# One core, a fused attention and convolution kernel: a new order of work on all five engines

## What is computed

```python
x = x + attention(gn(x))      # gn: group norm over 32 groups of 4 channels
x = x + conv(gn(x))

# attention: linear attention, 4 heads of 32 channels
xn  = h / max(norm of h over channels, 1e-12) * g * sqrt(128)
q, k, v = split(w_qkv @ xn)
q = softmax(q, over the head's 32 channels) * 32 ** -0.5
k = softmax(concat(mem_k, k), over the 4 + 4096 pixels)
out = w_out @ ((k v^T) q) + b_out

# conv: a 3 x 3 convolution over the channel pairs with (j - i) % 4 == 0,
# plus a 1 x 1 convolution over all the other pairs, plus a bias
```

## Time and profile before

| | |
|---|---|
| median of 3 runs | 2064.62 us (2064.17 to 2066.17) |
| profiled execution, its time | 2065.06 us |
| its span, first to last instruction | 2063.2 us |
| mean granted TensorE clock | 0.983 |
| TensorE busy | 1913.9 us (93%) |
| VectorE busy | 1750.3 us (85%) |
| ScalarE busy | 1354.0 us (66%) |
| GpSimd busy | 1362.4 us (66%) |

### The profile page before, as it was taken

The page is one execution under the profiler, slowest core; times in us unless marked ns, Lnnn a source line. Parts: engine busy times, 40 slices in busy tenths (PEclk is TensorE's granted clock), DMA queues, the critical chain, the costliest instruction groups (busy, mean ns, idle before and its releaser), DMA issues.

```text
span 2063.2 us, 50607 instructions
## 1 busy us (share of the span) xinstructions
PE 1913.9 (93%) x21199; PEld 1013.4 (49%) x21199; DVE 1750.3 (85%) x3144; ACT 1354.0 (66%) x1476; POOL 1362.4 (66%) x737
## 2 busy tenths in 40 slices
PE   2889999999999999999999999999999999999996
PEld 0445445555445555444555544555544555554552
DVE  5689888888988888988888988888988888898863
ACT  2567666767667767667676766676766776766761
POOL 5566666766667766667676667676666676666762
PEclk9789999999999999999999999999999999999997
DMA  5357777887767887667787777778777778876665
GB/s 105 62 127 147 154 149 158 168 169 153 149 154 160 169 168 158 151 148 160 169 158 165 154 152 153 162 164 173 149 151 151 159 168 171 154 151 147 144 136 127
DMA packets 349427, 312.96 MB, mean 152 GB/s; under 512 B 299152, under 2 KB 299920, under 8 KB 341008
## 3 DMA queue, kind: packets, MB, share of 16 engines
q1 hardware_dynamic: 347712, 308.73, 72.1%
q10 hardware_dynamic: 1168, 0.98, 0.2%
q0 software_dynamic: 320, 0.01, 0.0%
HBM read 68.10 MB, written 67.11 MB: 66 GB/s over the span
## 4 chain that ended last, share of the span: by engine, by line
PE 45%; DVE 36%; ACT 12%; POOL 3%; issue 1%; DMA 1%; ACTq 0%; SPq 0%
PE pair_ps L765 8%; DVE km L1114 7%; DVE u L1111 7%; PE pair_ps L802 7%; PE pair_ps L745 5%; DVE image L1166 4%; DVE nrm L1101 4%; DVE parts L1101 3%; PE bank_ps L699 3%; POOL exp_kT_lo L447 3%; PE bank_ps L775 3%; PE pair_ps L768 3%; PE pair_ps L793 3%; DVE part L1100 2%; PE bank_ps L754 2%; PE bank_ps L757 2%
## 5 line engine op out<-in xcount | busy, mean ns | idle before, releaser
L802 PE MATMUL pair_ps<-replicas,w_rep 96*32 96x512 f16 x8192 | 488.9, 383 | 7.9 <-DMA replicas<-yg_lo 7.9
L444 POOL TENSOR_TENSOR u_lo<-u,u_hi 128x1024 f16<-128x1024 f32 x128 | 269.9, 2144 | 270.3 <-ACT u_hi L551 270.3
L447 POOL TENSOR_TENSOR exp_kT_lo<-exp_kT,exp_kT_hi 128x1024 f16<-128x1024 f32 x128 | 300.2, 2354 | 178.9 <-ACT exp_kT_hi L560 178.8
L802 PEld LDWEIGHTS pair_ps<-replicas,w_rep 96*32 96x32 f16 x8192 | 205.8, 96 | 263.2 <-issue 77.8
L450 POOL TENSOR_TENSOR u_lo<-exp_q,u_hi 128x1024 f16<-128x1024 f32 x128 | 272.7, 2143 | 88.8 <-ACT u_hi L566 85.3
L1166 DVE SCALAR_TENSOR_TENSOR image<-pair_ps,image 128x512 f32<-128x512 f32 x256 | 172.5, 682 | 123.5 <-PE pair_ps L802 119.8
L440 POOL TENSOR_SCALAR u<-image,st 128x1024 f32<-128x1024 f32 x128 | 187.4, 1475 | 109.2 <-DVE st L1065 109.2
L551 ACT ACTIVATE u_hi<-u 128x1024 f16<-128x1024 f32 x128 | 130.8, 1045 | 173.3 <-DVE u L1111 173.1
L557 ACT ACTIVATE exp_kT<-pair_ps,zcol 128x1024 f32<-128x1024 f32 x128 | 141.0, 1102 | 144.0 <-PE pair_ps L745 144.0
L566 ACT ACTIVATE u_hi<-exp_q 128x1024 f16<-128x1024 f32 x128 | 135.3, 1057 | 137.1 <-DVE exp_q L1153 130.5
L536 ACT ACTIVATE exp_kT<-u,zcol 128x1024 f32<-128x1024 f32 x128 | 146.0, 1143 | 93.2 <-POOL u L440 92.2
(11 more groups left out here) (179 smaller groups left out, 4716.5 us busy)
## 6 DMA issues: line engine op xcount, KB each, us to landing
image<-in_x SPq DMA_DIRECT2D x256, 256.0 KB, 4.8
out<-image SPq DMA_DIRECT2D x512, 128.0 KB, 2.2
replicas<-yg_hi SPq DMA_DIRECT2D x256, 165.0 KB, 3.9
replicas<-yg_hi SPq DMA_DIRECT2D x256, 107.2 KB, 5.1
replicas<-yg_lo SPq DMA_DIRECT2D x128, 165.0 KB, 4.4
replicas<-yg_lo SPq DMA_DIRECT2D x128, 107.2 KB, 3.8
uT_hi<-u_hi SPq DMA_TRANSPOSE x128, 3.4
uT_lo<-u_lo SPq DMA_TRANSPOSE x128, 3.4
```

Of the source, the lines that this page charges most:

```text
L444: pool.tensor_tensor(px(UL, v), px(U, v), px(UH, v), ALU.subtract).then_inc(ul_ready, 1)
L447: pool.tensor_tensor(KL[:, v % 2], KT[:, v % 2], KH[:, v % 2], ALU.subtract).then_inc(kl_ready, 1)
L802: mm = pe.matmul(conv_ps[32 * r:32 * r + 32, j % 2], w_rep[0:32 * SLOTS, tap, r], rep[:, j * ROWS + dy:(j + 1) * ROWS + dy, dx:dx + SIDE], ...
```

## The change

Only the order of the calls in the five `step` functions changes, with the waits and the choice of PSUM banks that go with it. No helper is altered, and the number of instructions per image is the same. The core of the diff, cut; image names as above.

TensorE, head of the step: `conv_ring` of chunk 5 comes over from the step before, `inv_norm(…, 2)` goes to the end of the step before, and `rough_q` 0 and 1 stand around `turn_k_max`.

```diff
             def step(p, a, c, e):
                 if a is not None:
-                    pe.wait_ge(u_ready, at(a, UNITS, 1))
-                    inv_norm(a, 2, pair_ps[0])
-                if e is not None:
-                    pe.wait_ge(out_ready, at(e, CHUNKS, 5))
-                    conv_dense(e, 6)
-                if a is not None:
                     pe.wait_ge(u_ready, at(a, UNITS, 2))
                     inv_norm(a, 3, pair_ps[1])
                 if e is not None:
-                    conv_ring(e, 6)
+                    conv_ring(e, 5)
...
+                    conv_ring(e, 6)
                 if a is not None:
                     pe.wait_ge(k_max, at(a, 8, 1))
                     pe.wait_ge(uh_ready, at(a, UNITS, 3))
                     rough_k(a, 2, pair_ps[0])
+                if e is not None:
+                    pe.wait_ge(out_ready, at(e, CHUNKS, 6))
+                    conv_dense(e, 7)
+                if a is not None:
                     pe.wait_ge(k_max, at(a, 8, 2))
                     pe.wait_ge(uh_ready, at(a, UNITS, 4))
                     rough_k(a, 3, pair_ps[1])
                 if e is not None:
                     conv_ring(e, 7)
                 if a is not None:
+                    pe.wait_ge(k_max, at(a, 8, 4))
+                    rough_q(a, 0, pair_ps[1])
                     pe.wait_ge(k_max, at(a, 8, 7))
-                    turn_k_max(bank_ps[0])
-                    rough_q(a, 0, pair_ps[1])
+                    turn_k_max(bank_ps[1])
+                    rough_q(a, 1, pair_ps[0])
+                    pe.wait_ge(ul_ready, at(a, UNITS, 1))
+                    pe.wait_ge(k_max, at(a, 8, 8))
+                    keys(a, 0, pair_ps[2])
```

TensorE, from the second group means to the end of the step (new lines and the kept ones between them; "..." for the rest):

```diff
+                    context(a, 3, bank_ps[0])
...
+                    pe.wait_ge(lo_even, at(c, UNITS // 2, 1))
+                    conv_dense(c, 0)
+                    conv_dense(c, 1)
...
+                    turn_context(bank_ps[1])
...
+                    pe.wait_ge(hi_in[0], at(c, 16 * 2 * RES, 16 * 2 * RES))
+                    pe.wait_ge(lo_in[0], at(c, 16 * RES, 16 * RES))
+                    conv_ring(c, 0)
+                    conv_ring(c, 1)
...
+                    pe.wait_ge(den_dve, at(a, 4, 4))
+                    den_broadcast(a, 0, pair_ps[1])
+                    den_broadcast(a, 1, pair_ps[0])
...
+                    pe.wait_ge(out_ready, at(c, CHUNKS, 1))
                     conv_dense(c, 2)
...
+                    value_context(bank_ps[0])
...
                     pe.wait_ge(sq_ready, at(p, UNITS, 1))
                     norm_sums(p, 0, bank_ps[1])
...
                     pe.wait_ge(sq_ready, at(p, UNITS, 2))
                     norm_sums(p, 1, bank_ps[1])
...
+                    pe.wait_ge(q_soft, at(a, UNITS, 2))
+                    den_broadcast(a, 2, pair_ps[0])
+                    den_broadcast(a, 3, pair_ps[1])
                     pe.wait_ge(mix_dve, at(a, 9, 7))
                     mix_weights(bank_ps[0])
...
+                    conv_ring(c, 2)
...
+                    conv_ring(c, 4)
...
+                    pe.wait_ge(norm_dve, at(p, 5, 5))
+                    inv_norm(p, 0, pair_ps[0])
...
+                    pe.wait_ge(out_ready, at(c, CHUNKS, 4))
+                    conv_dense(c, 5)
...
                     inv_norm(p, 1, pair_ps[1])
...
+                    pe.wait_ge(out_ready, at(c, CHUNKS, 5))
+                    conv_dense(c, 6)
...
+                    pe.wait_ge(u_ready, at(p, UNITS, 1))
+                    inv_norm(p, 2, pair_ps[0])
```

```diff
+                    dve.wait_ge(max_turned, at(a, 2, 2))
+                    rows_q(a, bank_ps[1])
                 if p is not None and not first(p):
                     dve.wait_ge(x_in[0][buffer_of(p)], at_load(p))
                     x_stats(p, 0)
-                if a is not None:
-                    dve.wait_ge(max_turned, at(a, 2, 2))
-                    rows_q(a, bank_ps[1])
+                    x_stats(p, 1)
+                    dve.wait_ge(x_in[1][buffer_of(p)], at_load(p))
+                    x_stats(p, 2)
+                    x_stats(p, 3)
                 if c is not None:
                     dve.wait_ge(hi_ready, at(c, UNITS, 1))
                     dve.wait_ge(yg_ready, at(c, UNITS, 1))
                     low_y(c, 0)
...
                     x_seed(p, bank_ps[1])
+                    dve.wait_ge(x_stat, at(p, X_STEPS, 8))
+                    x_scale(p)
```

ScalarE: the squares of image a's units 0 to 2 end the step; `high_y(c, 3)` stands behind `square(p, 0)`; `norm_log` stands ahead of `high_q(a, 3)`. GpSimd: `low_u` 0 ends the step before, all four `group_norm_y` come first, and `low_k(a, 2)` comes before `low_y(c, 1)`:

```diff
-                    pool.wait_ge(yg_ready, at(c, UNITS, 2))
-                    pool.wait_ge(hi_ready, at(c, UNITS, 2))
-                    low_y(c, 1)
+                    group_norm_y(c, 2)
+                    group_norm_y(c, 3)
                 if a is not None:
                     pool.wait_ge(kh_ready, at(a, UNITS, 3))
                     low_k(a, 2)
                 if c is not None:
-                    group_norm_y(c, 2)
+                    pool.wait_ge(hi_ready, at(c, UNITS, 2))
+                    pool.wait_ge(yg_ready, at(c, UNITS, 2))
+                    low_y(c, 1)
```

More of the change, by code:

```diff
@@ L368, in step @@
                 if a is not None:
+                    sp.wait_ge(ul_ready, at(a, UNITS, 2))
+                    turn_u(a, 1)
+                if p is not None and p >= PRELOADED:
+                    if e is not None:
+                        sp.wait_ge(stored[2], at(e, 16 * RES, 16 * RES))
+                    if e is not None:
+                        sp.wait_ge(stored[3], at(e, 16 * RES, 16 * RES))
+                    load(p, 1)
+                if a is not None:
                     sp.wait_ge(ul_ready, at(a, UNITS, 3))
                     turn_u(a, 2)
-                if p is not None and p >= PRELOADED:
-                    if e is not None:
-                        sp.wait_ge(stored[3], at(e, 16 * RES, 16 * RES))
-                    if e is not None:
-                        sp.wait_ge(stored[2], at(e, 16 * RES, 16 * RES))
-                    load(p, 1)
+                    sp.wait_ge(ul_ready, at(a, UNITS, 4))
+                    turn_u(a, 3)
                 if c is not None:
@@ L382, in step @@
                     replicate_low(c, 0)
-                if a is not None:
-                    sp.wait_ge(ul_ready, at(a, UNITS, 4))
-                    turn_u(a, 3)
-                if c is not None:
                     sp.wait_ge(hi_ready, at(c, UNITS, 4))
@@ L393, in step @@
                     store(c, 0)
+                    sp.wait_ge(out_ready, at(c, CHUNKS, 4))
+                    store(c, 1)
             over_samples(step, replicate_weights)
@@ L514, in step @@
                     low_q(a, 3)
+                if p is not None:
+                    pool.wait_ge(uh_ready, at(p, UNITS, 1))
+                    low_u(p, 0)
             over_samples(step)
@@ L639, in step @@
                     square(p, 0)
+                if c is not None:
+                    high_y(c, 3)
+                if p is not None:
                     act.wait_ge(xg_ready, at(p, UNITS, 2))
@@ L658, in step @@
                     high_q(a, 2)
+                if p is not None:
+                    act.wait_ge(norm_dve, at(p, 5, 1))
+                    norm_log()
+                if a is not None:
                     act.wait_ge(q_soft, at(a, UNITS, 4))
@@ L670, in step @@
                     square_y(a, 0)
+                    act.wait_ge(y_ready, at(a, UNITS, 2))
+                    square_y(a, 1)
+                    act.wait_ge(y_ready, at(a, UNITS, 3))
+                    square_y(a, 2)
+                if p is not None:
+                    act.wait_ge(u_ready, at(p, UNITS, 1))
+                    high_u(p, 0)
             act.wait_ge(setup_pe, 1)
@@ L867, in step @@
[L867 to L874 removed]
                     pe.wait_ge(kT_exp, at(a, UNITS, 1))
                     pe.wait_ge(ul_ready, at(a, UNITS, 3))
[L877 removed]
+                    keys(a, 2, pair_ps[2])
@@ L878, in step @@
+                    pe.wait_ge(q_max, at(a, 5, 3))
+                    rough_q(a, 3, pair_ps[1])
                     pe.wait_ge(kT_exp, at(a, UNITS, 2))
-                    rough_q(a, 2, pair_ps[2])
+                    pe.wait_ge(ul_ready, at(a, UNITS, 4))
+                    keys(a, 3, pair_ps[0])
+                    if c is not None:
+                        pe.wait_ge(y_stat, at(c, Y_STEPS, 9))
+                    pe.wait_ge(kl_ready, at(a, UNITS, 1))
                     pe.wait_ge(uT_in[0], at(a, 32, 32))
-                    pe.wait_ge(kl_ready, at(a, UNITS, 1))
@@ L1184, in step @@
                     max_k(a, 1, pair_ps[1])
+                if e is not None:
+                    dve.wait_ge(conv_done, at(e, CHUNKS, 7))
+                    finish(e, 6)
+                if a is not None:
                     dve.wait_ge(k_rough, at(a, UNITS, 3))
@@ L1190, in step @@
                     shift_k(a)
+                if e is not None:
+                    dve.wait_ge(conv_done, at(e, CHUNKS, 8))
+                    finish(e, 7)
+                if a is not None:
```

(15 more changed lines are left out.)

282 lines of the change are left out of this document (108 added, 174 removed).

## The result

| | before | after |
|---|---|---|
| median (runs) | 2065.39 us (4; 2064.17 to 2067.15) | 2013.02 us (4; 2011.28 to 2016.92) |
| profiled execution, its time | 2065.06 us | 2011.88 us |
| mean granted TensorE clock | 0.983 | 0.983 |

The ratio is 0.9748, 95% interval 0.9731 to 0.9766: 52 us faster, where 61 were forecast (2004 us, range 1980 to 2072). In the new kernel the lines of TensorE's and VectorE's helpers are 10 or 11 higher: `conv_ring` L813, `broadcast` L717, `norm_sums` L710, `turn_k_max` L822, `group_means` L819, `turn_context` L828, `low_y` L1171 on VectorE. GpSimd's are 3 lower: `low_y` L454.

What follows compares the result with a forecast made beforehand. TensorE's own work was taken as the floor: 57.5 us plus waits of 1.0, 0.3, 0.3 and 0.2 is 59.3, rounded-away parts make 59.4; gain 1.96 x 31 = 61 us, from 2065.06 to 2004 us, range 1980 to 2072.

Steps and rivals of the forecast that it cites:

- Work without waits, 57.5: TensorE's work per period: 61.36 less 3.3 of waits is 58.1, adjusted for new neighbours to 57.5 us.
- The joined `norm_sums`: On TensorE, norm_sums 0 and 1 become adjacent and one call is free: -1.0 us a period.
- A change of shape: Whole-array matmuls directly ahead of a group on part of the array: 0.1 us each, +0.4 a period, bounds 0 and 0.8.
- Four broadcasts run as one: Rival on TensorE's den_broadcast pairs: each adjacent pair gains 0.3 us, period 58.8, 1986 us; chance 0.18.
- Head of the step, 1.0: TensorE's waits before inv_norm 3 (0.5), the shift of the keys (0.25) and keys 0 (0.2): together 1.0 us a period.
- the shift of the keys: VectorE's shift_k, 1.2 us, ends its head chain at 11.65; TensorE, free at 11.4, waits 0.25 us.
- Low parts and the port: VectorE's low_y 0 runs 27.9 to 29.0, then GpSimd's low_y 1; group means possible at 29.7, wanted at 30.5: no wait.
- the rival 0.12: VectorE misses its turn: statistics end after 27.9, GpSimd goes first, group means +1.35 us; period 60.45, 2037 us; chance 0.12.
- Replicas, 0.3: Last replica of the first band lands at 37.3; TensorE is at ring 0 at 37.0: wait 0.3 us, bounds 0 and 2.5.
- `norm_sums` 3, 0.3: Second half of the step: square 3 is done at 47.3, TensorE is there at 47.0: wait 0.3 us.
- End, 0.2: VectorE has norm_parts, two finish and residual 3 between ring 3 and inv_norm 0: TensorE waits 0.2 us.
- The last image: Its convolution lies outside the 31 periods; order was said hardly to matter there, so no change was counted.

Runs made afterwards that it cites:

- e3: The changed kernel with x_moments ahead of low_y 0, and den_broadcast 1 and 3 moved apart from 0 and 2: 2021.91 us, ratio 0.9791 to before.
- e9: The changed kernel with x_moments first, low_y 0 between x_stats 1 and 2, transposes earlier on the queue, plus low_y 2 behind den_parts: 2074.86 us, 1.0042 of before.
- e10: The changed kernel with x_moments first, low_y 0 between x_stats 1 and 2, transposes earlier, plus ring 5 back in its own step: 2049.8 us, 0.994 of before.
- e5: The changed kernel with x_moments ahead of low_y 0, and GpSimd's second group norm waiting for weigh_context: 2025.78 us, ratio 0.9809 to before.
- e8: The changed kernel with x_moments first, low_y 0 between x_stats 1 and 2, transposes earlier, plus GpSimd's group_norm_x 1 waiting for weigh_context: 2029.18 us, 0.9815 of before.

## Why the prediction was right, and where its terms were off

The forecast was 9 us low. Its main mechanism was right: TensorE's old waits at the head of the step are gone, and what decides next are short waits at other places. The step that failed is the walk of the low parts at the port, and several terms of the sum were off both ways. By its own steps:

- *Work without waits, 57.5.* The joined `norm_sums` do run in 1.06, as it said. A change of shape does cost 0.1 (the slot of `mix` 2 ends at 338.58, ring 3 starts at 338.67). Four broadcasts run as one, which it charged in full: -0.6 (e3: +0.50 to undo it). That rival was right.
- *Head of the step, 1.0.* `inv_norm` 3 waits 0.55 (0.5 forecast); `turn_k_max` waits 0.0 (0.25) and `keys` 0 0.1 (0.2). I took 1.2 for the shift of the keys from the earlier trace rows, but in it stood a port wait: the instruction on two columns took 0.70 there, and takes 0.17 in after, where GpSimd is done by then. The term was 0.35 too high.
- *Low parts and the port.* "GpSimd's next began when VectorE's had ended" holds in 17 periods and fails in 13, at 1.36 each: 13 x 1.36 / 30 = +0.6 on the mean. With the broadcasts this is the largest error, and the one that made the forecast low. I gave the rival 0.12 and a condition, statistics later than 27.9; mostly they ended at 26.8, a us early, and it still happened. The condition explains 3 of the 13.
- *`turn_context`.* It has no term. `weigh_context` waits at the port, and ring 0 starts some 0.5 late.
- *Replicas, 0.3.* The last one lands at 37.1 on average where 37.3 was taken. Since ring 0 was late itself, it waits in 8 periods only, 0.13 on the mean of all.
- *`norm_sums` 3, 0.3.* It is 0.7: what four-as-one and the joined sums bring reaches `square` 3 as a wait.
- *End, 0.2.* There is none.
- *The last image* was counted at no change and took 2.7 us more; by the record its waits grew from 16.8 to 18.6 us, and the rest I did not follow up.

The steady period without a missed turn and without a wait for the replicas is then 59.4 - 0.6 - 0.35 + 0.5 + 0.4 - 0.3 - 0.2 = 58.85, which is what the shortest periods show. With 0.6 for the missed turns, 0.13 for the replicas and 0.1 for the longer first periods it is 59.7, against 59.66. That the period came so near to 59.4 is luck: errors of 0.6 each way cancelled. Of the 9 us, 6 are the periods' (55.4 against 61), 2 the two ends', and 1 lies between the profiled execution and the median.

Why the 10 steps lose the turn with VectorE standing ready isn't settled. By the trace VectorE's `low_y` starts at 26.82 in periods that win it and in periods that lose it, 0.78 us before GpSimd's instruction ends. The Trainium skill ("SBUF — State Buffer", section Who interferes with whom) gives the shared pair of ports to whichever starts first, for its whole instruction. That fits the rows shown here in which one of them is running; it leaves open who is next when both stand ready, and so do these runs. When TensorE's clock falls behind a wait isn't settled either: it isn't the length of the wait alone (e9, e10).

## What to carry to other kernels

Time gained on the bounding engine is kept only as far as the next thing that didn't move: look a few us ahead for it (here `square` 3 took 0.6 of 1.0) before adding the gain up. Put what another engine waits for ahead of a large VectorE instruction that may have to share the port with GpSimd, and don't count on VectorE being next; a wait that is removed at the port can appear at the next meeting, and larger (three times here: e5, e8, e9). Where DMA issues share one queue, send what is ready and needed soon (transposes) ahead of what nobody waits for (stores).
